# Four graph layers on one core: node stages without GpSimd, one sum accumulator, and VectorE reading one operand from PSUM beside indirect DMAs

## The chip, the cores and the metric

The kernel runs on one core of a Trainium2 chip. The metric is device time in microseconds (us), the median of the runs; lower is better. PE is TensorE, DVE VectorE, ACT ScalarE, POOL GpSimd, SP SyncE (it issues plain DMAs).

## The reference

A graph with 6250 nodes of 128 features and 100000 edges, sorted by destination, goes through four residual layers: `x = x + layer(relu(layernorm(x)))`.

```
layer 0  msg = x[dst] * fsum(edge);  agg = segment_sum(msg, src)
         out = gamma * (softplus(agg @ Wi1 + bi1) @ Wi2 + bi2 - mean) * rsqrt(var) + beta
layer 1  twice: h = x @ W; e = exp(leaky(h.a_src[src] + h.a_dst[dst]) - max)
         x = layernorm(x + segment_sum(h[src] * e / sum(e)) + bias) * gamma + beta
layer 2  m = segment_sum(relu([x[src], edge_attr, g] @ Wm1 + bm1) @ Wm2 + bm2) / degree
         out = layernorm(x + relu([x, m, g] @ Wu1 + bu1) @ Wu2 + bu2) * ln_g + ln_b
layer 3  as layer 1 once, with 8 heads of 16 features, no layernorm, + bias
```

In layers 1 and 3 each node also has an edge to itself, and the weights of a node's incoming edges sum to one.

## The kernel before

**Nodes.** They lie in SBUF as 52 tiles of 128 (`NBP`), in 13 groups of 4 (`NG`, `GN`): `X` is the residual, `XI` and `Y` are scratch, `ACC` and `H` have 136 words per node (`AW`). `H` holds the rows that go to the table in HBM.

**Edges.** Setup gives each edge a slot. The edges of one destination tile fill whole tiles of 128 slots, so the last tile of each is partly empty, and behind the last edge some tiles are wholly empty: 832 tiles (`NT`), in 104 halves of 8 (`G`). The record of a slot has the edge's attributes, its source node (`R_SRC`) and its places. Setup first fills all records from `pad_rec`; there the source of an empty slot is 0.

**Passes.** `layer0_dst_pass`: for each half DVE builds eight one-hot tiles (`onehot`, L1055) from `iota_row`, PE picks the node rows with them, DVE scales them (L1175), POOL scatters them by 8 indirect DMAs (L1267), SP stores the one-hots. At its end DVE adds `bn_shift` to `X` (L1204). `layer0_src_pass` sums those messages by source. `gat_pass` runs three times (layer 1 twice, layer 3), `mlp_pass` once: in each half POOL gathers 8 tiles of table rows by 8 indirect DMAs (L1359) into one of four buffers (`ring`, `DEEP`), waiting for PE's sum of four halves before; DVE waits for all 8, works out the logits (L1469 to L1475) and the previous half is added up (`add_sums`); ACT takes exp and, with one head, scales the rows (L1503); with 8 heads DVE multiplies the rows by the weights (L1481); PE sums by destination into PSUM. `add_sums` adds the 8 PSUM tiles alternately into `ACC` and `H` (`sums`, L1102), each add waiting for the one two before it. So every node stage behind a pass first adds `H` to `ACC`.

**Beside a pass.** Before the first half DVE runs `meanwhile`: in `gat_pass` it is `self_loops`, which scales `H` (the whole node table) by the self weights in `den` (L1673).

**Node stages.** `node_product` turns and multiplies 13 groups; DVE's part is `before(g)` (layer 1's second product: gamma and beta, L1753 and L1754) and `after`; SP stores the table rows; POOL runs `behind(g)` (L1667), which adds a bias to `XI` or `X`. Behind the two passes of layer 1 stands `end1`: DVE adds `H` to `ACC` for 32 tiles (L1780), then normalizes and adds `XI` tile by tile (L1782), and takes statistics of all 52 (L177), while POOL does the other 20 tiles (`pool1`). `mean2` (L1816, L1817) prepares layer 2's product. The last stage ends with `finish`: three operations (L1688, L1689, L1851) on each of four parts, three of 12 tiles on DVE and one of 16 on POOL, each followed by the part's DMA to the output.

The order between engines is set by semaphores alone; stages end with a barrier.

Of the kernel before, what the change touches and what calls it, by code (L numbers as in the profile page):

```python
# [25 lines left out]
P = 128  # L26
N = 6250
E = 100000
D = 128
# [62 lines left out]
def gnn(nc, a, out):  # L92
# [28 lines left out]
    with ctx:  # L121
# [33 lines left out]
        for v in ("L1_gnn_bias", "L1_gnn_gamma", "L1_gnn_beta"):  # L155
            for l in range(2):
                vec[v, l] = (sb(f"{v}{l}", [P, D]), a[v][l, :])
        mat = {"Wi1": (sb("Wi1", [P, D]), a["L0_gnn_Wi1"]), "Wi2": (sb("Wi2", [P, D]), a["L0_gnn_Wi2"]),
# [53 lines left out]
        def setup():  # L212
# [63 lines left out]
            with stage_of_work():  # L276
# [25 lines left out]
                NW = len(vec) + len(mat) + 7 + 9  # L302
                with nc.Block() as block:
                    @block.sync
                    def _(sp):
# [11 lines left out]
                        for t, v in vec.values():  # L317
                            sp.dma_start(t[:, :], v.unsqueeze(0).to_broadcast([P, D])).then_inc(weights_in, 16)
                        for t, v in mat.values():
                            sp.dma_start(t[:, :], v).then_inc(weights_in, 16)  # L320
# [52 lines left out]
                    def _(pool):  # L373
# [15 lines left out]
                        st.then(pool.memset(zero1[:, :], 0.0))  # L389
                        pool.sem_inc(consts, 1)  # L390
# [6 lines left out]
                        st.then(pool.memset(pr[:, :, R_POS:R_POS + 1], float(SKIP)))  # L397
                        st.then(pool.memset(pm[:, :, D:D + 1], -1.0))
# [347 lines left out]
        def per_col(t):  # L746

            return t[:, :].unsqueeze(1).to_broadcast([P, NBP, D])
# [344 lines left out]
        def add_sums(dve, n, q, places, tiles, w, summed, signals, added):  # L1093
# [14 lines left out]
        def layer0_dst_pass():  # L1108
# [9 lines left out]
            with nc.Block() as block:  # L1118
# [32 lines left out]
                def _(dve):  # L1151
# [33 lines left out]
                    dve.wait_ge(cleared, 2)  # L1185
# [18 lines left out]
                    nc.vector.tensor_tensor(X[:, :, :], X[:, :, :], per_col(bn_shift), ALU.add)  # L1204
# [68 lines left out]
        def layer0_src_pass():  # L1273
# [14 lines left out]
            with nc.Block() as block:  # L1288
# [40 lines left out]
                def _(dve):  # L1329
# [4 lines left out]
                        add_sums(dve, i * deep + q, q, two_sets, acc_of_s, D, summed, i * deep + q + 1, added)  # L1334
# [47 lines left out]
        def gat_pass(table, heads, meanwhile):  # L1382
# [10 lines left out]
            maxed, reduced, asked, exped, parts_ready, sums_cleared = (  # L1393
                sem(n) for n in ("maxed", "reduced", "asked", "exped", "parts_ready", "sums_cleared"))
# [23 lines left out]
            def picks(q):  # L1418

                return bank[q % 2][:, 0:G * 6 * heads]  # L1420

# [4 lines left out]
            with nc.Block() as block:  # L1426
# [24 lines left out]
                def _(dve):  # L1451
# [3 lines left out]
                    dve.wait_ge(exped, 1)  # L1455
                    meanwhile(nc.vector, then)
                    dve.wait_ge(sums_cleared, 1)

                    def half(r, q, n):
# [3 lines left out]
                        if known(n, 2):  # L1463
                            dve.wait_ge(probs, n - 1)
# [11 lines left out]
                        if known(n, 1):  # L1476
                            add_sums(dve, n - 1, q - 1, two_sets, acc_of_d, w, pe_done, n + 1, added)
                        if heads > 1:
                            dve.wait_ge(probs, n + 1)
# [6 lines left out]
                    add_sums(dve, HALVES - 1, DEEP - 1, two_sets, acc_of_d, w, pe_done, HALVES + 1, added)  # L1486

                @block.scalar
                def _(act):
                    for q in range(DEEP):  # L1490
                        copy_index(0, q, ix_ready)
                    nc.scalar.copy(ACC[:, :, :], zero1[:, :].unsqueeze(2).to_broadcast([P, NBP, AW])).then_inc(sums_cleared, 1)
                    act.wait_ge(asked, 1)
                    nc.scalar.activation(ps_self, ps_self, ACT.Exp, bias=zero1[:, :]).then_inc(exped, 1)
# [16 lines left out]
                def _(pe):  # L1511
# [14 lines left out]
                    def half(r, q, n):  # L1526
                        pe.wait_ge(logits, n + 1)
# [7 lines left out]
        def mlp_pass(table, meanwhile):  # L1535
# [10 lines left out]
            with nc.Block() as block:  # L1546
# [22 lines left out]
                def _(dve):  # L1569
                    def half(r, q, n):  # L1570
# [6 lines left out]
                        if known(n, 1):  # L1577
                            add_sums(dve, n - 1, q - 1, one_set, acc_of_d, w, summed, n, added)
# [6 lines left out]
                    add_sums(dve, HALVES - 1, DEEP - 1, one_set, acc_of_d, w, summed, HALVES, added)  # L1585
# [68 lines left out]
        def gat_product(l, heads, table, addends, normed, before=None):  # L1654
# [9 lines left out]
            def behind(g):  # L1664

                for t, row_vec in addends:
                    nc.gpsimd.tensor_tensor(t[:, group(g), :], t[:, group(g), :], columns(row_vec, GN), ALU.add)  # L1667
            node_product([XI], [wx[l]], after, before, normed, cols=cols, store=(table, H, D + heads), behind=behind)

        def self_loops(v, then, heads):  # L1670

            ps, h4 = by_head(den, heads), H[:, :, 0:D].rearrange("p b (k c) -> p b k c", k=heads)
            then(v.tensor_tensor(h4, h4, ps.unsqueeze(3).to_broadcast([P, NBP, heads, D // heads]), ALU.mult))  # L1673
            then(v.tensor_copy(H[:, :, D:D + heads], ps))

        def weights_of_nodes(v, then, heads):

            at = slice(D, D + heads)
            then(v.tensor_tensor(by_head(den, heads), ACC[:, :, at], H[:, :, at], ALU.add))  # L1679
            if heads == 8:  # L1680
                then(v.tensor_scalar(by_head(den, heads), by_head(den, heads), 1e-16, None, ALU.add))  # L1681
            then(v.reciprocal(by_head(den, heads), by_head(den, heads)))  # L1682

        def rows_of_nodes(v, then, tiles, heads):
# [3 lines left out]
            then(v.tensor_tensor(ACC[:, tiles, 0:D], ACC[:, tiles, 0:D], H[:, tiles, 0:D], ALU.add))  # L1688
# [67 lines left out]
        for l in range(2):  # L1756
            with stage_of_work():
                addends = [(XI, vec["L1_gnn_bias", l][0])]
                if l == 0:
                    gat_product(0, 1, tab_d[0], addends, relu_norm_x)  # L1760
                else:
                    addends.append((X, vec["L1_gnn_beta", 1][0]))
                    gat_product(1, 1, tab_d[1], addends, lambda g: scaled(g, ACT.Identity, Y), norm_l1)
                gat_pass(tab_d[l], 1, lambda v, then: self_loops(v, then, 1))
                weights_in_den = sem("weights_in_den")
                cut = NBP - 20
                assert cut % 2 == 0

                def pool1(pool, v, then):
                    tiles = slice(cut, NBP)  # L1770
                    then(v.tensor_tensor(ACC[:, tiles, 0:D], ACC[:, tiles, 0:D], H[:, tiles, 0:D], ALU.add))
                    pool.wait_ge(weights_in_den, 1)
                    then(v.tensor_tensor(ACC[:, tiles, 0:D], ACC[:, tiles, 0:D],
                                         by_head(den, 1)[:, tiles, :].to_broadcast([P, NBP - cut, D]), ALU.mult))
                    then(v.tensor_tensor(Y[:, tiles, :], ACC[:, tiles, 0:D], XI[:, tiles, :], ALU.add))

                def end1(d, v, then):
                    weights_of_nodes(v, then, 1)
                    d.dve.sem_inc(weights_in_den, 1)
# [118 lines left out]
```

## Time and profile before

| | us |
|---|---|
| time, median of 3 runs (lowest, highest) | 7642.42 (7634.22, 7653.16) |
| profiled execution: its own time | 7654.14 |
| its span in the trace | 7652.4 |
| busy in the span: PE, PEld, DVE, ACT, POOL | 3341.1, 2964.8, 3135.5, 1683.9, 5276.8 |
| TensorE clock granted, mean share of full speed | 0.636 |

PEld is TensorE's weight load. Busy time alone doesn't name a limit; what each stage waits for does. The stages by time of the trace: setup to about 1300, layer 0's destination pass to 2490, its source pass and product to 2857, then product and pass in turn: passes at 2897 to 3969, 4085 to 5155, 5267 to 6331 and 6507 to 7611, and the last node stage to the end.

### The profile page before, as it was taken

Reading aid. Unit: us, or ns where it says so; the run is one execution under the profiler, and the core shown is the slowest. Engines: PE = TensorE matmul, PEld = TensorE weight load, DVE = VectorE, ACT = ScalarE, POOL = GpSimd, SP = SyncE. Lnnn points to the kernel's source line nnn. Section 1 sums busy time; section 2 is a strip of 40 time slices with the busy share of each in tenths; the row PEclk is TensorE's granted clock in tenths of the full one; section 3 lists DMA queues with packets and bytes.
Section 4 is the critical chain, followed back from the end, with each engine's and each line's share of the span. In section 5 each row is a group of like instructions: output and inputs, shape, how many; then the busy total and the mean of one; then the engine's idle time right before and its main releaser. Section 6 shows DMA issues by size and latency. Waiting matters only on the chain. (4 is left out here: it accounts for less than half of the span.)

```text
span 7652.4 us, 88779 instructions
## 1 busy us (share of the span) xinstructions
PE 3341.1 (44%) x17325; PEld 2964.8 (39%) x17326; DVE 3135.5 (41%) x10255; ACT 1683.9 (22%) x4072; POOL 5276.8 (69%) x5234
## 2 busy tenths in 40 slices
PE   3100001444443764444434444444777675454543
PEld 1000001444443653444423444434666664344443
DVE  9777721222222663222244222225222326444444
ACT  3100000111111863222223222223222224000000
POOL 2677776777777737777756777764777770777775
PEclk9655555666666985555655555556777777566565
DMA  6122234444443624444443444453444451444444
GB/s 218 63 94 94 94 105 152 144 143 142 141 143 113 215 84 133 131 131 131 131 73 109 131 131 131 131 101 91 134 137 134 133 120 29 127 128 132 128 132 93
DMA packets 507506, 942.53 MB, mean 123 GB/s; under 512 B 204348, under 2 KB 240684, under 8 KB 507305
## 3 DMA queue, kind: packets, MB, share of 16 engines
q1 hardware_dynamic: 349288, 637.41, 24.8%
q0 software_dynamic: 158144, 304.31, 17.7%
q8 instruction: 26, 0.43, 0.0%
q14 instruction: 48, 0.39, 0.0%
HBM read 673.90 MB, written 270.84 MB: 123 GB/s over the span
## 5 line engine op out<-in xcount | busy, mean ns | idle before, releaser
L1359 POOL DMA_INDIRECT edge_buf<-node_table,ixr x1664 | 1614.4, 970 | 596.4 <-issue 506.7
L1359 POOL DMA_INDIRECT Y<-node_table,ixr x1664 | 1587.1, 954 | 507.4 <-issue 507.4
L1267 POOL DMA_INDIRECT layer_messages<-edge_buf,ixr x832 | 911.0, 1095 | 295.5 <-issue 263.8
L431 POOL DMA_INDIRECT edge_records<-edge_buf x782 | 792.2, 1013 | 255.6 <-issue 245.8
L1517 PE MATMUL bank<-adc,turned_buf 128*128 x2496 | 341.7, 194 | 1304.2 <-DVE z L1475 916.9
L1089 PE MATMUL bank<-edge_buf,Y 128*128 128x129 f32 (+2 forms) x3744 | 817.2, 404 | 213.4 <-ACT edge_buf L1503 104.8
L1469 DVE TENSOR_REDUCE pk<-bank 128x16 f32<-128x48 f32 (+1 forms) x312 | 101.3, 325 | 1883.4 <-DMA edge_buf<-node_table,ixr 946.2
L1089 PE MATMUL bank<-Y 128*128 128x129 f32 (+1 forms) x3328 | 758.3, 418 | 247.5 <-ACT Y L1503 130.1
L1089 PEld LDWEIGHTS bank<-edge_buf,Y 128*128 128x128 f32 x3744 | 756.1, 306 | 242.2 <-issue 120.2
L1517 PEld LDWEIGHTS bank<-adc,turned_buf 128*128 128x128 bf16 x2496 | 256.9, 103 | 1445.5 <-issue 1390.0
L1089 PEld LDWEIGHTS bank<-Y 128*128 128x128 f32 x3328 | 704.8, 319 | 271.0 <-issue 218.4
L1102 DVE TENSOR_TENSOR ACC<-ACC,bank 128x129 f32 (+2 forms) x2080 | 605.9, 291 | 354.8 <-issue 265.3
L1102 DVE TENSOR_TENSOR H<-H,bank 128x129 f32 (+2 forms) x2080 | 599.4, 288 | 3.2 <-DVE ACC L1102 1.7
L1215 PE MATMUL bank<-ident,Y 128*128 128x128 f32 x832 | 204.3, 427 | 821.2 <-DVE Y L1055 819.0
L1215 PEld LDWEIGHTS bank<-ident,Y 128*128 128x128 f32 x832 | 163.2, 223 | 845.0 <-issue 649.6
L1636 PE MATMUL bank<-wmbT,turned_buf 64*128 64x128 f32 x1664 | 312.2, 361 | 297.7 <-DVE Y L1575 148.4
L1636 PEld LDWEIGHTS bank<-wmbT,turned_buf 64*128 64x128 f32 x1664 | 285.6, 264 | 326.0 <-issue 301.2
L480 PE MATMUL bank<-Y,H 128*128 128x2 f32 (+1 forms) x6 | 1.4, 358 | 774.1 <-DVEq L708 774.1
L1498 ACT ACTIVATE edge_buf<-z,zero 128x8 f32<-128x8 f32 (+1 forms) x156 | 50.2, 322 | 1303.2 <-DVE z L1475 1303.2
L1227 PE MATMUL bank<-H,Y 128*128 x1664 | 329.8, 382 | 5.4 <-DVEq L1180 5.4
L1227 PEld LDWEIGHTS bank<-H,Y 128*128 128x128 f32 x1664 | 328.6, 302 | 5.6 <-issue 5.6
L1498 ACT ACTIVATE Y<-z,zero 128x8 f32<-128x8 f32 (+1 forms) x156 | 50.1, 321 | 1272.3 <-DVE z L1475 1272.3
(284 smaller groups left out, 5386.7 us busy)
## 6 DMA issues: line engine op xcount, KB each, us to landing
Y<-onehots SPq DMA_DIRECT2D x416, 512.0 KB
turned_buf<-onehots_turned SPq DMA_DIRECT2D x312, 256.0 KB
edge_buf<-edge_records SPq DMA_DIRECT2D x208, 288.0 KB
onehots<-Y SPq DMA_DIRECT2D x104, 512.0 KB, 2.7
layer_messages<-ACC SPq DMA_DIRECT2D x28, 1584.0 KB
XI<-layer_messages SPq DMA_DIRECT2D x78, 528.0 KB, 4.3
edge_records<-H SPq DMA_DIRECT2D x1, 29952.0 KB
onehots_turned<-turned_buf SPq DMA_DIRECT2D x104, 256.0 KB
```

Of the source, the lines that this page charges most:

```text
L431: pool.indirect_dma_start(rec_d, bass.IndirectOffsetOnAxis(ap=ixs[h][:, j:j + 1], axis=0), rec[h][:, j, :], None, bounds_check=SLOTS - 1, ...
L480: nc.tensor.matmul(bank[5][:, 16 * l:16 * l + 2 * heads_of[l]], wT[l], att[l], start=True, stop=True).then_inc(wT_ready, 1)
L1089: ins = nc.tensor.matmul(places.at(q, j, w), tiles_of_half(onehots)[:, j, :], messages[:, j, 0:w], start=True, stop=True)
L1102: nc.vector.tensor_tensor(acc, acc, places.at(q, j, w), ALU.add).then_inc(added, 1)
L1215: ins = nc.tensor.transpose(bank[j // 4][:, (j % 4) * P:(j % 4) * P + P], tiles_of_half(oh[h])[:, j, :], ident[:, :])
L1227: ins = nc.tensor.matmul(bank[2 + j // 4][:, (j % 4) * P:(j % 4) * P + P], ohT[h][:, j * P:j * P + P], Hflat[:, bass.ds(at[j] * AW, D)], s ...
L1267: pool.indirect_dma_start(msg_d, bass.IndirectOffsetOnAxis(ap=ixr[h][:, j:j + 1], axis=0), rows[h][:, j, 0:MW], None, bounds_check=SLOTS - ...
L1359: pool.indirect_dma_start(ring[q][:, j, 0:w], None, table, bass.IndirectOffsetOnAxis(ap=ixr[q][:, j:j + 1], axis=0)).then_inc(rows_in[q], 16)
L1469: st.then(nc.vector.tensor_reduce(ps, picks(q).rearrange("p (j t k) -> p j k t", j=G, t=3), AX.X, ALU.add))
L1498: nc.scalar.activation(ring[q][:, :, D:w], z[q % 2][:, :, 0:heads], ACT.Exp, bias=zero1[:, :]) \
L1517: ins = nc.tensor.matmul(picks(q)[:, j * 6 * heads:(j + 1) * 6 * heads], ohbT[q][:, j * P:j * P + P], adc[:, bass.ds(at[j] * (6 * heads), ...
L1636: ins = nc.tensor.matmul(bank[2 + j // 4][:, (j % 4) * P:(j % 4) * P + P], attrT[q % 2][:, j * P:j * P + P], wmbT[:, :], start=True, stop= ...
```

## The change

1. `onehot`, the add of `bn_shift` (L1204), `self_loops` (L1673) and the 8-head product (L1481) read one input from PSUM. Copies of `iota_row` and `bn_shift` are put in banks 4 and 5; ACT writes the self weights and, with 8 heads, each half's weights a second time, into PSUM. With 8 heads PE's pick of two halves on now waits for DVE's product.
2. `add_sums` is given its list of accumulators. In `gat_pass` and `mlp_pass` it is `ACC` alone, so each add waits for the one before it; layer 0's source pass keeps both. `self_loops` writes to `ACC`, ACT's clearing of `ACC` goes, and so do all adds of `H` to `ACC` behind these passes.
3. No node stage uses POOL. Layer 1's bias is added where `H` is copied from PSUM (`bias_row`); the additions to `X` are made by DVE beside the pass (`add_row_to_x`). `end1` and `finish` do all tiles on DVE, the last part of `finish` with 16 tiles.
4. In `pad_rec` the source of slot (p, j) is row 8p + j instead of 0, by one POOL iota in setup.

```diff
@@ setup
+                        st.then(pool.iota(pr[:, :, R_SRC:R_SRC + 1], [[1, G], [1, 1]], base=0, channel_multiplier=G,
+                                          allow_small_or_imprecise_dtypes=True))
@@ onehot, layer0_dst_pass
-            return nc.vector.tensor_tensor(tiles_of_half(oh[h]), iota_row[:, :].unsqueeze(1).to_broadcast([P, G, P]),
+            return nc.vector.tensor_tensor(tiles_of_half(oh[h]), bank[4][:, 0:P].unsqueeze(1).to_broadcast([P, G, P]),
...
+                    nc.vector.tensor_copy(bank[4][:, 0:P], iota_row[:, :]).then_inc(cleared, 1)
+                    nc.vector.tensor_copy(bank[5][:, 0:D], bn_shift[:, :]).then_inc(cleared, 1)
...
-                    nc.vector.tensor_tensor(X[:, :, :], X[:, :, :], per_col(bn_shift), ALU.add)
+                    nc.vector.tensor_tensor(X[:, :, :], X[:, :, :], per_col(bank[5][:, 0:D]), ALU.add)
@@ add_sums
-                acc = sums[j % 2][:, bass.ds(at[j], w)]
-                if j >= 2 or known(n, 1):
-                    dve.wait_ge(added, n * G + j - 1)
+                acc = accs[j % len(accs)][:, bass.ds(at[j], w)]
+                if j >= len(accs) or known(n, 1):
+                    dve.wait_ge(added, n * G + j + 1 - len(accs))
@@ gat_pass
-                            dve.wait_ge(probs, n + 1)
+                            dve.wait_ge(probs, (n + 1) * exps)
...
-                                                    ring[q][:, :, D:w].unsqueeze(3).to_broadcast([P, G, heads, c]),
+                                                    weights(q).unsqueeze(3).to_broadcast([P, G, heads, c]),
...
-                    nc.scalar.copy(ACC[:, :, :], zero1[:, :].unsqueeze(2).to_broadcast([P, NBP, AW])).then_inc(sums_cleared, 1)
...
+                        if heads > 1:
+                            nc.scalar.activation(weights(q), z[q % 2][:, :, 0:heads], ACT.Exp, bias=zero1[:, :]) \
+                                .then_inc(probs, 1)
...
-                        pe.wait_ge(logits, n + 1)
+                        pe.wait_ge(*((msg_ready, n + 1) if heads > 1 else (logits, n + 1)))
@@ gat_product
-                v.tensor_copy(H[:, at, 0:D + heads], rows_psum[:, :, 0:D + heads])
+                if l < 2:
+                    v.tensor_tensor(H[:, at, 0:D + 1], rows_psum[:, :, 0:D + 1],
+                                    bias_row[l][:, :].unsqueeze(1).to_broadcast([P, 2, D + 1]), ALU.add)
+                else:
+                    v.tensor_copy(H[:, at, 0:D + heads], rows_psum[:, :, 0:D + heads])
...
-                    nc.gpsimd.tensor_tensor(t[:, group(g), :], t[:, group(g), :], columns(row_vec, GN), ALU.add)
+        def add_row_to_x(v, then, row):
+            in_psum = bank[7][:, 0:D]
+            then(v.tensor_copy(in_psum, row[:, :]))
+            then(v.tensor_tensor(X[:, :, :], X[:, :, :], per_col(in_psum), ALU.add))
@@ self_loops
-            then(v.tensor_tensor(h4, h4, ps.unsqueeze(3).to_broadcast([P, NBP, heads, D // heads]), ALU.mult))
+            then(v.tensor_tensor(acc4, h4, ps_psum.unsqueeze(3).to_broadcast([P, NBP, heads, D // heads]), ALU.mult))
@@ end1
-                    then(v.tensor_tensor(ACC[:, 0:cut, 0:D], ACC[:, 0:cut, 0:D], H[:, 0:cut, 0:D], ALU.add))
-                    for b in range(cut):
+                    for b in range(NBP):
@@ layer 2: after_h, mlp_pass, mean2
-                v.memset(ACC[:, b:b + 2, :], 0.0)
-                v.tensor_tensor(X[:, b:b + 2, :], X[:, b:b + 2, :], columns(vec["L2_gnn_ln_b"][0], 2), ALU.add)
...
-            mlp_pass(tab_d[2], lambda v, then: then(v.memset(H[:, :, :], 0.0)))
+            def beside2(v, then):
+                then(v.memset(ACC[:, :, :], 0.0))
+                add_row_to_x(v, then, vec["L2_gnn_ln_b"][0])
+            mlp_pass(tab_d[2], beside2)
...
-                then(v.tensor_tensor(ACC[:, at, 0:D], ACC[:, at, 0:D], H[:, at, 0:D], ALU.add))
@@ last stage
-                    for n in range(3):
+                    for n in range(4):
                         finish(dve, nc.vector, then, n)
-                @block.gpsimd
-                def _(pool):
-                    pool.wait_ge(den_ready, 1)
-                    finish(pool, nc.gpsimd, Steps(pool, pool_steps).then, 3)
```

## Rows read from the trace of the kernel before

**Rows 1.** Windows: length; busy (x) PE, PEld, DVE, ACT, POOL; PE clock; DMA; GB/s.

```profile
1312.00:2489.00 1177.00, 506.09 (x2464) 483.90 (x2464) 326.72 (x618) 210.08 (x410) 910.99 (x832) 0.65 0.41 139
...
5267.00:6310.00 1043.00, 739.97 (x4112) 682.97 (x4112) 308.83 (x1018) 236.79 (x416) 787.25 (x832) 0.73 0.48 134
6506.00:7588.00 1082.00, 517.24 (x2464) 456.85 (x2464) 458.03 (x1435) 45.58 (x207) 826.51 (x833) 0.59 0.47 127
```

**Rows 2.** The scatters' source line: duration ns min/median/max; who waited for them (us, times).

```profile
L1267 POOL DMA_INDIRECT layer_messages<-edge_buf,ixr x832: 971/974/8733, 1312.7 to 2486.9; - x167
...
  DVE edge_buf L1168: 760.6, 102
```

**Rows 3.** Timeline of the destination pass, DVE and POOL: start us, duration us, engine, line.

```profile
1761.38 1.29 DVE L1175 TENSOR_TENSOR edge_buf<-bank,XI 128x512 f32<-128x512 f32 x2
1762.45 0.97 POOL L1267 DMA_INDIRECT layer_messages<-edge_buf,ixr  x1 [0.30 <-issue]
...
1763.54 1.22 DVE L1055 TENSOR_TENSOR Y<-iota_row,XI 128x1024 f32<-128x1024 f32 x1
1763.73 1.88 POOL L1267 DMA_INDIRECT layer_messages<-edge_buf,ixr  x1 [0.30 <-issue]
...
2462.51 8.73 POOL L1267 DMA_INDIRECT layer_messages<-edge_buf,ixr  x1 [0.30 <-DVE edge_buf L1175]
...
2463.32 7.07 DVE L1204 TENSOR_TENSOR X<-X,bn_shift 128x6656 f32<-128x6656 f32 x1
```

**Rows 4.** Timeline, start of layer 1's first pass and a half of layer 3's.

```profile
2900.16 7.09 DVE L1673 TENSOR_TENSOR H<-H,den 128x6656 f32<-128x6656 f32 x1
2900.28 7.79 POOL L1359 DMA_INDIRECT edge_buf<-node_table,ixr  x1 [0.30 <-issue]
...
7005.36 1.22 DVE L1481 TENSOR_TENSOR Y<-Y 128x1024 f32<-128x1024 f32 x1
7006.23 1.17 POOL L1359 DMA_INDIRECT Y<-node_table,ixr  x1 [0.30 <-issue]
```

**Rows 5.** Timeline, last gather of a half and DVE's start on it: mid-pass, then the end.

```profile
3403.68 0.94 POOL L1359 DMA_INDIRECT edge_buf<-node_table,ixr  x1 [0.30 <-issue]
...
3406.28 0.21 DVE L1469 TENSOR_REDUCE pk<-bank 128x16 f32<-128x48 f32 x1 [4.57 <-DMA edge_buf<-node_table,ixr]
...
3944.06 0.94 POOL L1359 DMA_INDIRECT Y<-node_table,ixr  x1 [0.30 <-issue]
...
3958.36 0.21 DVE L1469 TENSOR_REDUCE pk<-bank 128x16 f32<-128x48 f32 x1 [9.55 <-DMA Y<-node_table,ixr]
```

**Rows 6.** DMA queues, 3500 to 3600, then 3930 to 3960: packets, MB, share of 16 engines.

```profile
q0 software_dynamic: 2558, 5.29, 23.9%
...
q0 software_dynamic: 542, 1.10, 82.6%
```

**Rows 7.** Groups of the second layer-1 product, 4013 to 4073: busy us, mean ns, idle before.

```profile
L1753 DVE TENSOR_TENSOR XI<-XI,L_gnn_gamma 128x512 f32<-128x512 f32 x13 | 20.1, 1547 | 6.4 <-ACT XI L1695 4.8
...
L1754 DVE TENSOR_TENSOR XI<-XI,L_gnn_beta 128x512 f32<-128x512 f32 x13 | 18.4, 1416 | 0.4
```

**Rows 8.** `end1`: group of L1780, timeline of L1782, its durations (min/median/max ns).

```profile
L1780 DVE TENSOR_TENSOR ACC<-ACC,H 128x4096 f32<-128x4096 f32 x2 | 8.8, 4424 | 0.3
...
3973.85 23.49 DVE L1782 SCALAR_TENSOR_TENSOR Y<-ACC,den,XI 128x128 f32<-128x128 f32 x32
...
3985.57 11.51 DVE L1782 SCALAR_TENSOR_TENSOR Y<-ACC,den,XI 128x128 f32<-128x128 f32 x23
...
L1782 DVE SCALAR_TENSOR_TENSOR Y<-ACC,den,XI x64: 337/339/5736, 3973.9 to 5184.3; 128x128 f32<-128x128 f32 x64
```

**Rows 9.** The group that `mean2` loses.

```profile
L1816 DVE TENSOR_TENSOR ACC<-ACC,H 128x512 f32<-128x512 f32 x13 | 9.0, 691 | 2.3 <-PEq L761 0.5
```

**Rows 10.** Timeline of the last stage: L1851 on the first and the third part.

```profile
7618.45 5.94 DVE L1851 TENSOR_TENSOR X<-X,ACC 128x1536 f32<-128x1536 f32 x1
...
7641.03 1.76 DVE L1851 TENSOR_TENSOR X<-X,ACC 128x1536 f32<-128x1536 f32 x1
```

More of the change, by code:

```diff
@@ L154, in gnn @@
             vec[v] = (sb(v, [P, D]), a[v])
-        for v in ("L1_gnn_bias", "L1_gnn_gamma", "L1_gnn_beta"):
+        for v in ("L1_gnn_gamma", "L1_gnn_beta"):
             for l in range(2):
                 vec[v, l] = (sb(f"{v}{l}", [P, D]), a[v][l, :])
+        bias_row = [sb(f"L1_gnn_bias{l}", [P, D + 1]) for l in range(2)]
         mat = {"Wi1": (sb("Wi1", [P, D]), a["L0_gnn_Wi1"]), "Wi2": (sb("Wi2", [P, D]), a["L0_gnn_Wi2"]),
@@ L389, in _ @@
                         st.then(pool.memset(zero1[:, :], 0.0))
+                        for t in bias_row:
+                            st.then(pool.memset(t[:, D:D + 1], 0.0))
                         pool.sem_inc(consts, 1)
@@ L1652, in _, with gat_product @@
                     each_half(pe, half)
-        def gat_product(l, heads, table, addends, normed, before=None):
+        def gat_product(l, heads, table, normed, before=None):
             ad = by_head(a_dst, heads)
@@ L1670, in self_loops @@
+                then(v.tensor_copy(ad[:, at, :], rows_psum[:, :, D + heads:cols]))
+            node_product([XI], [wx[l]], after, before, normed, cols=cols, store=(table, H, D + heads))
+        def add_row_to_x(v, then, row):
+            in_psum = bank[7][:, 0:D]
+            then(v.tensor_copy(in_psum, row[:, :]))
+            then(v.tensor_tensor(X[:, :, :], X[:, :, :], per_col(in_psum), ALU.add))
         def self_loops(v, then, heads):
             ps, h4 = by_head(den, heads), H[:, :, 0:D].rearrange("p b (k c) -> p b k c", k=heads)
-            then(v.tensor_tensor(h4, h4, ps.unsqueeze(3).to_broadcast([P, NBP, heads, D // heads]), ALU.mult))
@@ L1674, in self_loops @@
-            then(v.tensor_copy(H[:, :, D:D + heads], ps))
+            acc4 = ACC[:, :, 0:D].rearrange("p b (k c) -> p b k c", k=heads)
+            ps_psum = bank[7][:, 0:NBP * heads].rearrange("p (b k) -> p b k", k=heads)
+            then(v.tensor_tensor(acc4, h4, ps_psum.unsqueeze(3).to_broadcast([P, NBP, heads, D // heads]), ALU.mult))
+            then(v.tensor_copy(ACC[:, :, D:D + heads], ps))
         def weights_of_nodes(v, then, heads):
-            at = slice(D, D + heads)
-            then(v.tensor_tensor(by_head(den, heads), ACC[:, :, at], H[:, :, at], ALU.add))
+            weights = ACC[:, :, D:D + heads]
@@ L1680, in weights_of_nodes @@
             if heads == 8:
-                then(v.tensor_scalar(by_head(den, heads), by_head(den, heads), 1e-16, None, ALU.add))
-            then(v.reciprocal(by_head(den, heads), by_head(den, heads)))
+                then(v.tensor_scalar(by_head(den, heads), weights, 1e-16, None, ALU.add))
+                weights = by_head(den, heads)
+            then(v.reciprocal(by_head(den, heads), weights))
         def rows_of_nodes(v, then, tiles, heads):
@@ L1687, in rows_of_nodes @@
             acc4 = ACC[:, tiles, 0:D].rearrange("p b (k c) -> p b k c", k=heads)
-            then(v.tensor_tensor(ACC[:, tiles, 0:D], ACC[:, tiles, 0:D], H[:, tiles, 0:D], ALU.add))
             then(v.tensor_tensor(acc4, acc4, by_head(den, heads)[:, tiles, :].unsqueeze(3)
@@ L1757, in gnn, with beside1 @@
             with stage_of_work():
-                addends = [(XI, vec["L1_gnn_bias", l][0])]
                 if l == 0:
-                    gat_product(0, 1, tab_d[0], addends, relu_norm_x)
+                    gat_product(0, 1, tab_d[0], relu_norm_x)
                 else:
[L1762 to L1775, printed above, removed]
+                    gat_product(1, 1, tab_d[1], lambda g: scaled(g, ACT.Identity, Y), norm_l1)
+                def beside1(v, then):
+                    self_loops(v, then, 1)
+                    if l == 1:
+                        add_row_to_x(v, then, vec["L1_gnn_beta", 1][0])
+                gat_pass(tab_d[l], 1, beside1)
                 def end1(d, v, then):
                     weights_of_nodes(v, then, 1)
-                    d.dve.sem_inc(weights_in_den, 1)
-                    then(v.tensor_tensor(ACC[:, 0:cut, 0:D], ACC[:, 0:cut, 0:D], H[:, 0:cut, 0:D], ALU.add))
-                    for b in range(cut):
+                    for b in range(NBP):
                         ins = v.scalar_tensor_tensor(Y[:, b, :], ACC[:, b, 0:D], den[:, b:b + 1], XI[:, b, :], ALU.mult, ALU.add)
                     then(ins)
-                    for b in range(cut):
-                        ins = count_stats(v, b, Y)
-                    d.wait_pool()
-                    for b in range(cut, NBP):
+                    for b in range(NBP):
                         ins = count_stats(v, b, Y)
@@ L1790, in end1 @@
                     finish_stats(v, then, d.root)
-                Dense(end1, roots=1, on_pool=pool1)
+                Dense(end1, roots=1)
                 if l == 1:
@@ L1840, in gnn, with beside3 @@
         with stage_of_work():
-            gat_product(2, 8, tab_d[3], [(X, vec["L3_gnn_bias"][0])], relu_norm_x)
-            gat_pass(tab_d[3], 8, lambda v, then: self_loops(v, then, 8))
-            den_ready, written, steps, pool_steps = (sem(n) for n in ("den_ready", "written", "steps", "pool_steps"))
+            gat_product(2, 8, tab_d[3], relu_norm_x)
+            def beside3(v, then):
+                self_loops(v, then, 8)
+                add_row_to_x(v, then, vec["L3_gnn_bias"][0])
+            gat_pass(tab_d[3], 8, beside3)
+            written, steps = sem("written"), sem("steps")
             parts = [slice(n * GN * 3, (n + 1) * GN * 3) for n in range(3)] + [slice(GN * 9, NBP)]
```

40 lines of the change are left out of this document (21 added, 19 removed).

## The prediction, made before the changed kernel ran

> **What bounds the kernel now.** I read the windows first, to see which engine each stage keeps busy, then the timeline for what that engine does there. In layer 0's destination pass POOL is busy 911 of 1177 us, in the MLP pass 787 of 1043, in the 8-head pass 827 of 1082; no other engine comes near in the first and last [rows 1]. The timeline tells what fills POOL's rest: 0.30 us of issue between one indirect DMA and the next, and no wait for anyone [rows 3, 4]. So a pass lasts as long as POOL takes for 832 DMAs: 0.974 + 0.30 us each for a scatter [rows 2], 787.25/832 = 0.946 + 0.30 for a gather [rows 1]. DVE has room: in the destination pass it waits 761 us for scatters to land, 7.5 us in each of 102 halves [rows 2]. Between the passes DVE sets the pace. The change therefore pays only where it shortens one of POOL's DMAs, what follows the last of them, or DVE's own list in a node stage.
>
> **POOL held up by DVE.** One scatter in eight is long. The one that starts at 1763.73 beside a one-hot (two inputs in SBUF) takes 1.88 us and ends 0.85 us after it; the one that starts at 1762.45 while L1175 runs (one input PSUM) takes its ordinary 0.97 [rows 3]. The same holds for L1673, 7.09 us long, with a gather of 7.79, for L1481, and for L1204 [rows 3, 4]. The reading: a DMA whose start falls into a DVE operation with two SBUF inputs waits for its end, one beside a PSUM input doesn't.
> - Destination pass: 910.99 - 832 x 0.974 = 100.6 us over the plain length. Of it 8.73 - 0.97 = 7.8 is L1204's; a short cast in front of it may keep some 0.7, the pass's first DMA another 0.6. Saved: 99 us, 92 of it by the one-hots.
> - `self_loops`: 7.79 - 0.95 = 6.8 us in each of three passes, 20.5 us.
> - 8-head product: 826.51 - 787.25 (the MLP pass, which has no such operation) = 39.3; less 0.4 for the reduction in that window, 6.8 counted above and about 2 for small operations at the start that stay: 30 us.
>
> Bounds: all of it as long as one PSUM input is enough, nothing if it isn't. I take the upper end, since L1175 is the same form of operation (PSUM times SBUF) and ran 208 times in this very pass. The new copies into PSUM and the second exp stand where DVE and ACT wait, 0.2 to 0.6 us each. One sentence from the Trainium skill speaks against it: "SBUF — State Buffer", Who interferes with whom, names a contention between two SBUF inputs and GpSimd instructions that read SBUF, but infers that a tensor_tensor leaves the writing of DMA descriptors alone. By that the long DMAs would have another cause and these 149.5 us stay; the rows with L1055 and L1673 disagree with it, and go before it.
>
> **The end of each pass.** Mid-pass DVE starts 3406.28 - (3403.68 + 0.94) = 1.66 us after a half's last gather; at the end 3958.36 - 3945.00 = 13.36 us [rows 5]. There the queue moves 1.10 MB in 30 us at 82.6% of the DMA engines' time, mid-pass 5.29 MB in 100 us at 23.9% [rows 6]: 5 times the time per byte. The last tiles are all empty slots, so every read goes to row 0. With different rows I expect the mid-pass lag: 11.7 us saved at each of four passes, 46 us. Bounds: nothing (rows a fixed step apart no better), 47. Mid-pass the slow reads of partly empty tiles are hidden behind POOL's issue and give nothing.
>
> **One accumulator.** Adds now follow each other. Two on different buffers start 0.21 us apart while one takes 0.29; dependent ones would start about 0.32 apart (0.29 and the 0.03 seen between dependent DVE operations). Eight: 0.9 us more. In a pass this goes into DVE's 7 us of waiting; on the path are six groups of eight (the last of the layer-1 passes, two each for the MLP and 8-head passes, where PE's sum or the product stands behind the adds): -5.3 us. Bounds: 0 to -14 (0.5 us apart). The 7 us add to `X` beside three passes delays the first half by up to 6 us, and four buffers of 10 us hide that; without that cover it would be 6 us each. ACT's clearing of `ACC` ended before it was needed.
>
> **Node stages.**
> - Layer 1's second product: L1753 and L1754 take 38.5 us for 26 operations beside POOL's additions [rows 7]; L1816, the same shape, needs 0.691 [rows 9]. 38.5 - 18.0 = 20.5 us. Bounds 15 (ACT, or the store of the table, is late next) and 26. The other products are paced by ACT and gain nothing.
> - `end1`: gone are L1780 (4.4 us) and 23.5 us for 32 L1782, three of them stuck behind POOL for up to 5.7; in come 52 at (11.51 - 5.74)/22 = 0.262 us, 13.6 [rows 8]. With the small add at its head 14.6 us, twice: 29 us. Bounds 27 and 30.
> - `mean2` loses 13 x 0.72 (0.691 and the gap) = 9.4 us, as DVE works there without a break [rows 9]. Bounds 6 and 9.4.
> - End: nine operations of 1536 columns, three of which POOL stretches from 1.76 to 5.0 or 5.9 [rows 10], about 27.4 us; then six of 1.76 and two of 2048 columns at about 2.3, 15.2 us. With fewer tiles behind the last of them to be sent, 14 us. Bounds 10 and 18.
>
> **Sum.** 99 + 20.5 + 30 + 46 - 5.3 + 20.5 + 29 + 9.4 + 14 = 263 us. The profiled execution took 7654.1 us, 11.7 above the median of its runs, so 7391 for one like it and 7642.4 - 263 = **7379 us** for the median.
>
> **The rivals.**
> - PSUM doesn't free POOL: the output or the remaining SBUF input is what blocks. For it: only small or half-length PSUM operations were seen beside POOL. Against it: 208 of L1175 without one long DMA that needs them. The 149.5 us stay: 7529 us. Chance 0.07. The inference quoted from the Trainium skill's "SBUF — State Buffer" would lead here.
> - Empty slots stay slow at a pass's end: the new rows stand 8 apart, a step near 4 KB in each table, and could meet in one part of HBM. Against it: mid-pass rows are spread at random and come at once, and 128 different rows can hardly be as bad as one. 46 us stay: 7425 us. Chance 0.08.
> - Slower: the dependent add. DVE's half in the 8-head pass is about 3.7 us and eight adds, in the layer-1 passes 2; in the MLP pass PE's sum (near 4 us) waits for the adds. From an add every 0.8 us (1.0 in layer 1) DVE and not POOL would pace all 416 halves, and from 0.96 it eats the whole gain; at 1.0 the time is about 7379 + 8 x 0.2 x 208 = 7712 with what the ends lose. For it: each add has a wait on a count in a register and an address from a register. Against it: they have both now, and start 0.21 us apart. Chance 0.03.
> - Something that no row shows, among it that nothing changes: 0.02.
>
> **How the numbers follow.** My forecast has 0.80, with 7355 to 7420 as its own range. The full range takes in the empty slots' case: 7340 to 7440; it leaves out the first and third rival. Within 0.3% (23 us, about what a measurement of this kernel tells from none) only partial failures of several kinds would end: 0.02. Slower 0.03, faster 0.95.
>
> **What would show it.** In the destination pass no scatter of 1.9 us, POOL's busy time near 812 us, the pass 1077 us long; in the 8-head pass POOL near 789; no gather of 7.8. At each pass's end DVE within 2 us of the last gather. L1753's successor at 0.69, 52 STT 0.26 apart, POOL absent between passes. It is wrong if long DMAs remain beside the one-hots, if adds start more than 0.5 us apart, or if POOL waits for PE's sums.

## The result and the profile after

The changed kernel takes **7409.4 us** (median of 4 runs, 7404.5 to 7412.4) against 7647.7 us (4 runs, 7634.2 to 7653.2): a ratio of 0.9688, interval 0.9677 to 0.9700, 238 us less. Predicted were 7379 us, 263 us less, with a range of 7340 to 7440. The profiled execution took 7404.5 us, span 7402.5: 249.9 us of span less than the profiled one of before. That difference is accounted for here, stretch by stretch, from the start of the first and the end of the last indirect DMA of each pass. The column "expected" puts the prediction's own terms into the stretches.

| stretch | before, us | after, us | difference | expected |
|---|---|---|---|---|
| start to first setup scatter | 242.2 | 250.5 | +8.3 | 0 |
| setup scatters, to first destination scatter | 1070.6 | 1069.4 | -1.2 | 0 |
| destination pass | 1175.1 | 1073.2 | -101.9 | -99 |
| to first gather of layer 1 | 409.7 | 411.7 | +2.0 | 0 |
| layer-1 passes | 1047.5, 1047.4 | 1038.5, 1038.3 | -9.0, -9.2 | -6.8 each |
| between them | 140.5 | 85.5 | -55.0 | -46 |
| second to MLP pass | 135.1 | 108.4 | -26.6 | -25 |
| MLP pass | 1040.7 | 1038.2 | -2.5 | 0 |
| MLP to 8-head pass | 198.4 | 174.9 | -23.6 | -19 |
| 8-head pass | 1079.5 | 1057.8 | -21.7 | -37 |
| last gather to the end | 65.8 | 56.1 | -9.6 | -24 |

Two stretches gave less than expected, the 8-head pass with what follows it and the start. Two gave clearly more: those in front of the second layer-1 pass and of the 8-head pass, where POOL begins with an all-reduce.

The windows of the destination, MLP and 8-head pass answer to [rows 1]:

```profile
1319.00:2394.00 1075.00, 494.82 (x2464) 473.51 (x2464) 327.00 (x619) 210.21 (x410) 809.29 (x832) 0.66 0.44 152
5075.00:6114.00 1039.00, 791.27 (x4144) 720.02 (x4144) 374.57 (x1027) 237.53 (x415) 784.95 (x832) 0.68 0.46 135
6288.00:7347.00 1059.00, 481.32 (x2440) 434.47 (x2440) 513.33 (x1429) 70.36 (x309) 786.56 (x833) 0.66 0.46 132
```

POOL's busy time in the first row is 809 where it was 911, in the third 787 where it was 827. But the third window is 20 us longer than the second at the same POOL work: POOL now waits there. The source line of the scatters (durations in ns: min, median, max) and the timeline beside a one-hot answer to [rows 2, 3]:

```profile
L1279 POOL DMA_INDIRECT layer_messages<-edge_buf,ixr x832: 969/972/1742, 1319.9 to 2392.2; - x167
```

```profile
1755.68 1.23 DVE L1064 TENSOR_TENSOR Y<-bank,XI 128x1024 f32<-128x1024 f32 x1
1755.94 0.97 POOL L1279 DMA_INDIRECT layer_messages<-edge_buf,ixr  x1 [0.30 <-issue]
...
2807.46 7.09 DVE L1702 TENSOR_TENSOR ACC<-H,bank 128x6656 f32<-128x6656 f32 x1
2807.58 0.95 POOL L1371 DMA_INDIRECT edge_buf<-node_table,ixr  x1 [0.30 <-issue]
```

The operations on DVE have the shapes and the lengths that they had (1.22 and 7.09 us, [rows 3, 4]). One input now comes from a bank, and the DMA that starts inside them takes 0.97 or 0.95 us, not 1.88 or 7.79. At the end of the first layer-1 pass, for [rows 5, 6]:

```profile
3842.39 0.94 POOL L1371 DMA_INDIRECT Y<-node_table,ixr  x1 [0.30 <-issue]
3844.97 0.21 DVE L1486 TENSOR_REDUCE pk<-bank 128x16 f32<-128x48 f32 x1 [5.15 <-DMA Y<-node_table,ixr]
...
3846.66 0.29 DVE L1111 TENSOR_TENSOR ACC<-ACC,bank 128x129 f32 x1 [0.64 <-issue]
```

```profile
q0 software_dynamic: 384, 0.79, 11.3%
```

DVE begins 1.64 us after the last gather, 13.36 before. The second view is the gathers' DMA queue from 3830 to 3858 (packets, MB, share of 16 engines). Share times window over MB gives 4.0 us for each MB; in the rows of before it is 4.5 mid-pass and 22.5 at the end. The groups of the second layer-1 product, then `end1`, then the first and last part of the last stage, for [rows 7, 8, 10]:

```profile
L1781 DVE TENSOR_TENSOR XI<-XI,L_gnn_gamma 128x512 f32<-128x512 f32 x13 | 9.0, 692 | 6.4 <-ACT XI L1723 4.8
L1782 DVE TENSOR_TENSOR XI<-XI,L_gnn_beta 128x512 f32<-128x512 f32 x13 | 9.0, 692 | 0.4
```

```profile
3857.09 13.74 DVE L1800 SCALAR_TENSOR_TENSOR Y<-ACC,den,XI 128x128 f32<-128x128 f32 x52
...
7381.79 1.76 DVE L1869 TENSOR_TENSOR X<-X,ACC 128x1536 f32<-128x1536 f32 x1
...
7393.43 2.29 DVE L1869 TENSOR_TENSOR X<-X,ACC 128x2048 f32<-128x2048 f32 x1
```

**Where the 8-head pass is bound now.** Two halves of it on DVE, PE and POOL:

```profile
7007.92 3.29 DVE L1111 TENSOR_TENSOR ACC<-ACC,bank 128x136 f32 x8 [4.19 <-PE bank L1098]
...
7011.12 1.21 DVE L1498 TENSOR_TENSOR edge_buf<-edge_buf,bank 128x1024 f32<-128x1024 f32 x1
...
7013.34 1.11 PE L1538 MATMUL bank<-adc,turned_buf 128*128 x8 [5.56 <-DVE edge_buf L1498]
...
7014.46 3.62 PE L1098 MATMUL bank<-edge_buf,Y 128*128 128x136 f32 x16
...
7018.22 3.29 DVE L1111 TENSOR_TENSOR ACC<-ACC,bank 128x136 f32 x8 [4.41 <-PE bank L1098]
...
7019.03 0.94 POOL L1371 DMA_INDIRECT edge_buf<-node_table,ixr  x1 [0.66 <-issue]
```

Read the releasers in brackets: the adds wait for PE's sums, the picks for the product, the product for the adds in front of it. That is a closed ring: adds 3.29, product 1.21 (it begins at the last add's end), 1.0 until PE picks, picks 1.12, sums 3.62, 0.14 until the next adds; 10.3 us from one half's adds to the next. From the eleventh half to the last few the products follow each other in 10.16 to 10.31 us, 10.24 in the mean. POOL needs 8 x (0.944 + 0.305) = 9.99. The ring is slower and first uses up the slack of the four buffers. After that POOL has to wait at the first DMA of a half, where its gap grows from 0.30 to as much as 0.69. Over the pass POOL's gaps sum to 271.6 us against 253.4 before. These first gaps make up 8.8 of the 18.2 us more. The rest comes in front of the second DMA of a half, nearly all of it in holes of 1.86 us that stand at every twelfth half from half 38 on. Holes of 1.84 to 1.88 us stand at every 112th scatter of the destination pass too, in both kernels. What makes any of them the traces don't tell; the ring keeps its 10.24 us through them. In before's trace eight adds took 1.79 us and the picks ran beside them.

### The profile page after: what moved, and what is told of

Read it like the earlier page. It is cut to its first block and busy times, and to the rows that moved or that the text cites. A ratio compares the mean times of both kernels' runs of the same rounds, so it can differ in the third digit from the quotient of the medians.

```text
span 7402.5 us, 89274 instructions
## 1 busy us (share of the span) xinstructions
PE 3331.8 (45%) x17325; PEld 2957.3 (40%) x17326; DVE 3299.0 (45%) x10231; ACT 1691.6 (23%) x4176; POOL 5000.4 (68%) x5176
## 5 line engine op out<-in xcount | busy, mean ns | idle before, releaser
L1371 POOL DMA_INDIRECT edge_buf<-node_table,ixr x1664 | 1571.6, 944 | 619.4 <-issue 507.9
L1371 POOL DMA_INDIRECT Y<-node_table,ixr x1664 | 1569.7, 943 | 521.1 <-issue 519.9
L1111 DVE TENSOR_TENSOR ACC<-ACC,bank 128x129 f32 (+2 forms) x3744 | 1092.9, 292 | 1102.2 <-PE bank L1098 469.2
L1279 POOL DMA_INDIRECT layer_messages<-edge_buf,ixr x832 | 809.3, 973 | 295.7 <-issue 263.0
L1657 PE MATMUL bank<-wmbT,turned_buf 64*128 64x128 f32 x1664 | 293.0, 345 | 192.3 <-DVE Y L1596 101.3
L1657 PEld LDWEIGHTS bank<-wmbT,turned_buf 64*128 64x128 f32 x1664 | 266.7, 248 | 224.6 <-issue 210.1
L1267 ACT COPY Y<-bank 128x512 f32<-128x512 f32 x208 | 123.8, 595 | 840.3 <-PE bank L1239 840.1
L1177 DVE COPY edge_buf<-XI 128x8 f32 (+1 forms) x104 | 18.7, 180 | 664.6 <-DMA layer_messages<-edge_buf,ixr 664.6
```

The source lines that it names most:

```text
L1177: nc.vector.tensor_copy(rows[h][:, :, D:D + 1], fields[:, bass.ds(t, G), R_SLOC - EA:R_SLOC - EA + 1]) \
L1267: nc.scalar.copy(ohT[h][:, at], bank[n][:, :]).then_inc(ohT_ready, 1)
L1279: pool.indirect_dma_start(msg_d, bass.IndirectOffsetOnAxis(ap=ixr[h][:, j:j + 1], axis=0), rows[h][:, j, 0:MW], None, bounds_check=SLOTS - ...
L1371: pool.indirect_dma_start(ring[q][:, j, 0:w], None, table, bass.IndirectOffsetOnAxis(ap=ixr[q][:, j:j + 1], axis=0)).then_inc(rows_in[q], 16)
L1657: ins = nc.tensor.matmul(bank[2 + j // 4][:, (j % 4) * P:(j % 4) * P + P], attrT[q % 2][:, j * P:j * P + P], wmbT[:, :], start=True, stop= ...
```

## The experiments

Experiments 1 to 4 ran on one chip (before there: 7651.8 us), the others on a second (7636.3), but for the all-reduce at the end in experiment 6, which ran on a third. There the kernel before takes 8980.7 us, and in that run POOL's gaps in a gather pass sum to 399 to 456 us and not 253; why that chip is slower was not looked into. So ratios are compared. Gathers take 0.944 us in some executions and 0.947 in others, with either kernel, which makes 2.0 to 2.5 us a pass; POOL's sums are compared with this in mind. Whole times step too: of experiment 1's four runs the profiled one, with 0.944, took 7367.6 us and the others 7383.0 to 7384.8; of experiment 7's five the profiled one, with 0.947, took 7368.6 and the others 7353.0 to 7354.4.

**1. Only the picks go back in front of the product.** For that the weights move to PSUM banks that the picks don't use.

```diff
-                return bank[q % 2][:, 384:384 + G * heads].rearrange("p (j k) -> p j k", k=heads)
+                return bank[4 + 3 * (q % 2)][:, 384:384 + G * heads].rearrange("p (j k) -> p j k", k=heads)
-                        pe.wait_ge(*((msg_ready, n + 1) if heads > 1 else (logits, n + 1)))
+                        pe.wait_ge(logits, n + 1)
```

> The changed kernel, with the 8-head weights moved from the picks' PSUM bank to one that the sums of the same half use, so that PE picks the half after next as soon as the logits are out again, ahead of the product. Theory (a ring: product on DVE, pick and sums on PE, eight dependent adds on DVE, 10.17 us a half against POOL's 9.97): the ring loses the pick's 1.15 us and falls below POOL, so the 8-head pass goes from 1057.8 to 1038-1042 us and the time from its last gather to the last add from 30.4 to 22-26; in all 20 to 26 us less than the 7409.4 of the changed kernel, about 7386. Rival (ACT's second exp, or something in POOL's own issue, makes the gaps): pass and total stay at 1058 and 7409.

Measured: 7383.4 us, ratio 0.9649 (0.9633 to 0.9665). Pass 1040.1 us, from the last gather to the last add 15.9 us (30.1 in the changed kernel; 24.0 before). The window of the pass:

```profile
6283.00:7324.00 1041.00, 512.06 (x2472) 453.16 (x2473) 529.02 (x1449) 71.03 (x312) 787.23 (x833) 0.60 0.46 134
```

```profile
7007.85 3.29 DVE L1111 TENSOR_TENSOR ACC<-ACC,bank 128x136 f32 x8 [0.80 <-issue]
7007.96 1.13 PE L1538 MATMUL bank<-adc,turned_buf 128*128 x8 [1.30 <-DVE z L1492]
...
7011.05 1.21 DVE L1498 TENSOR_TENSOR Y<-Y,bank 128x1024 f32<-128x1024 f32 x1
...
7012.36 3.97 PE L1098 MATMUL bank<-Y 128*128 128x136 f32 x16 [3.27 <-DVE Y L1498]
```

The picks run beside the adds, the sums follow the product by 0.1 us, and the adds no longer wait for PE. ACT's second exp and the slow adds are still there, so neither of them alone holds the pass up. The holes of 1.86 us are gone as well, here and in experiment 2. The ring had cost 17.7 us in the pass and 14.2 behind it.

**2. Only two accumulators again, in the 8-head pass.**

```diff
+            accs = sums if heads > 1 else sums[0:1]
-                            add_sums(dve, n - 1, q - 1, two_sets, sums[0:1], acc_of_d, w, pe_done, n + 1, added)
+                            add_sums(dve, n - 1, q - 1, two_sets, accs, acc_of_d, w, pe_done, n + 1, added)
                 self_loops(v, then, 8)
+                then(v.memset(H[:, :, :], 0.0))
```

with `H` added to `ACC` again behind the pass.

> The changed kernel, with two accumulators again in the 8-head pass alone (H cleared ahead of the pass, added in at the end: some 6 us of clearing that the buffers may hide, 0.6 and four times 1.8 us of adding behind the pass). Theory (the ring): adds start 0.21 us apart instead of 0.43, a half's ring is 8.7 us, POOL paces again: pass 1038-1042 us instead of 1057.8, from the last gather to the last add 24 to 26 us instead of 30.4, less 16 to 24 and plus 8, about 7395. Rival (pick behind the product is enough by itself to pace the pass): pass 1050 us or more, total 7409 or above.

Measured: 7389.2 us, ratio 0.9655 (0.9639 to 0.9671). Pass 1042.0 us, adds 0.21 us apart:

```profile
7024.10 0.30 DVE L1111 TENSOR_TENSOR ACC<-ACC,bank 128x136 f32 x1 [0.83 <-issue]
7024.31 0.29 DVE L1111 TENSOR_TENSOR H<-H,bank 128x136 f32 x1
...
7027.93 1.14 PE L1539 MATMUL bank<-adc,turned_buf 128*128 x8 [5.05 <-DVE Y L1499]
```

The late picks alone do no harm either. It takes both edits. Of the ring's 10.3 us the slow adds are 1.5 and the late picks 2.1; without either one it lies below POOL's 9.99 us.

**3. The kernel before, with only the one-hots' iota in PSUM.**

```diff
+                    nc.vector.tensor_copy(bank[4][:, 0:P], iota_row[:, :]).then_inc(cleared, 1)
-            return nc.vector.tensor_tensor(tiles_of_half(oh[h]), iota_row[:, :].unsqueeze(1).to_broadcast([P, G, P]),
+            return nc.vector.tensor_tensor(tiles_of_half(oh[h]), bank[4][:, 0:P].unsqueeze(1).to_broadcast([P, G, P]),
```

> The kernel before, with one edit: the one-hots of layer 0's destination pass take iota from PSUM. Theory (a DVE operation with two SBUF inputs holds up POOL's DMA, one PSUM input frees it): no scatter of 1.88 us is left but the one beside L1204, the pass goes from 1175 to about 1083 us, in all 92 us less: 7556. Rival (the output or the remaining SBUF input is what blocks, and the changed kernel gains elsewhere): 7648.

Measured: 7559.9 us, ratio 0.9878 (0.9861 to 0.9894). The pass took 1082.3 us, 92.8 less:

```profile
1313.00:2397.00 1084.00, 507.35 (x2464) 484.89 (x2464) 327.18 (x617) 209.88 (x409) 817.79 (x832) 0.66 0.44 151
```

```profile
L1268 POOL DMA_INDIRECT layer_messages<-edge_buf,ixr x832: 971/974/8736, 1313.6 to 2394.9; - x167
```

Of 100.6 us over the plain length 7.4 are left; the scatter beside the addition to `X` still takes 8.74 us. So where one operand lies decides. Its length, its output and its other input are as they were.

**4. The kernel before, with only different rows in the empty slots.**

```diff
+                        st.then(pool.iota(pr[:, :, R_SRC:R_SRC + 1], [[1, G], [1, 1]], base=0, channel_multiplier=G,
+                                          allow_small_or_imprecise_dtypes=True))
```

> The kernel before, with one edit: empty slots name 1024 different rows instead of row 0. Theory (one row read by all is slow, different rows are not): DVE starts 1.7 us after the last gather at all four pass ends instead of 13.4, 46 us less: 7602. Rival (the ends got shorter through the other edits): 7648. On the start: the changed kernel's POOL stood still for 9.3 us at its second instruction; if this iota brings that about, the first setup scatter comes at 250 us and not at 242.

Measured: 7603.4 us, ratio 0.9935 (0.9918 to 0.9951), 48 us less. DVE starts 1.6 to 1.7 us after the last gather at all four ends:

```profile
3942.22 0.95 POOL L1361 DMA_INDIRECT Y<-node_table,ixr  x1 [0.31 <-issue]
3944.78 0.21 DVE L1471 TENSOR_REDUCE pk<-bank 128x16 f32<-128x48 f32 x1 [6.64 <-DMA Y<-node_table,ixr]
```

The first setup scatter comes at 242.1: this iota has nothing to do with the changed kernel's late start.

**5. One row for each DMA of a half.** As 4, with `channel_multiplier=0`.

> The kernel before, with one edit: empty slots name eight different rows, by their tile in the half, so that all 128 of a DMA's reads still go to one row, but the eight DMAs of a half to eight. If what is slow is the reading of one row by all 16 engines, DVE starts less late than 13.4 us where DMAs overlap: with one row a DMA I expect 5 to 13 us after the last gather; with no difference between rows (rows of a table as near as these meet in one place), 13.4. If only the whole queue's meeting in a single row were slow, 1.7.

```profile
3937.75 0.94 POOL L1361 DMA_INDIRECT Y<-node_table,ixr  x1 [0.30 <-issue]
3941.54 0.21 DVE L1471 TENSOR_REDUCE pk<-bank 128x16 f32<-128x48 f32 x1 [6.79 <-DMA Y<-node_table,ixr]
```

Measured: DVE starts 2.6 to 2.9 us after the last gather at the four ends. I had expected 5 to 13. There is one run, of 7601.5 us, too few to read a difference in time from. All 128 reads of a DMA in one row cost only 1.2 us; what cost 11.7 was a queue of DMAs that all read the same one.

**6. The start and the all-reduces.** POOL's first instructions in the changed kernel:

```profile
0.80 0.20 POOL L380 MEMSET ident<- 128x128 f32 x1 [0.29 <-POOLq L1898]
10.55 0.28 POOL L381 TENSOR_SCALAR_AFFINE_SELECT ident<-ident 128x128 f32<-128x128 f32 x1 [9.54 <-issue]
```

Before, the select starts at 1.49. And the all-reduce in front of the second layer-1 pass, first before, then after:

```profile
4076.66 0.25 DVE L1398 TENSOR_REDUCE gmax<-H 128x1 f32<-128x52 f32 x1 [4.27 <-PEq L822]
...
4084.98 0.38 POOL L1445 PARTITION_ALL_REDUCE gmax_all<-gmax  x1 [8.65 <-issue]
```

```profile
3927.69 0.24 DVE L1410 TENSOR_REDUCE gmax<-H 128x1 f32<-128x52 f32 x1 [3.59 <-PEq L831]
...
3928.09 0.39 POOL L1463 PARTITION_ALL_REDUCE gmax_all<-gmax  x1 [84.76 <-DVEq L1411]
```

The 8 us are gone there and in front of the 8-head pass, and stay in front of the first layer-1 pass (2795.94 to 2804.27), where POOL's last work was 104 TENSOR_TENSOR instructions in layer 0's source pass. In the traces POOL's sequencer has a MODIFY_POOL_CONFIG pair at its start, with or without a standstill there, and wherever its work changes between all-reduce and TENSOR_TENSOR, and nowhere else. In the kernel before, POOL's parts of `end1` and of the last stage start 6.8, 6.9 and 7.1 us behind such a pair too. That led to a theory: POOL holds the code of one kind of instruction, and a swap costs 7 to 9 us. Two edits on top of experiment 1, and one on the kernel before, test it. The first, in the last stage:

```diff
+                @block.gpsimd
+                def _(pool):
+                    nc.gpsimd.tensor_tensor(gmax[:, :], gmax_all[:, :], gmax_all[:, :], ALU.add)
```

> The changed kernel with the early pick (7383.4 us), and one small POOL addition in the last stage, beside DVE's work there. Theory (POOL keeps the code it ran last, an all-reduce needs another one than additions and selects, a swap takes 7 to 9 us, and an execution starts with what the last one left): the swap happens at the end, where POOL has nothing to do, and the 9.0 to 9.3 us standstill at POOL's first select is gone; first setup scatter at 242 instead of 250 us, in all 8 us less, about 7375. The addition waits some 7 us for the swap, DVE's last work takes 19: nothing is lost there. Rival (the standstill comes from the size or place of the changed kernel's code): the first scatter stays at 250 us, total 7383.

Measured: 7360.4 us, ratio 0.9637 (0.9622 to 0.9652). First setup scatter at 242.1, and

```profile
1.49 0.29 POOL L381 TENSOR_SCALAR_AFFINE_SELECT ident<-ident 128x128 f32<-128x128 f32 x1 [0.49 <-POOL ident L380]
```

The second, early in the first layer-1 product, beside DVE's and PE's work:

```diff
+                    nc.gpsimd.partition_all_reduce(gmax_all[:, 0:1], zero1[:, :], P, bass.bass_isa.ReduceOp.max)
```

> The changed kernel with the early pick (7383.4 us), and one all-reduce of a column of zeros on POOL early in the first layer-1 product, whose result nobody uses. Theory (swap of POOL's code): POOL swaps beside the product, the real all-reduce of that stage starts at once and not 8.3 us late, from the last destination scatter to the first gather 403 us instead of 411.4, in all 8 us less, about 7375. Rival (the all-reduce itself takes 8 us the first time, or waits for something of DVE): the real one is late as before, total 7383.

Measured: 7362.0 us, ratio 0.9639 (0.9624 to 0.9654); from the last scatter to the first gather 404.3 us (411.4 in experiment 1):

```profile
2769.70 0.38 POOL L1682 PARTITION_ALL_REDUCE gmax_all<-zero  x1 [106.24 <-DVEq L814]
2796.47 0.39 POOL L1463 PARTITION_ALL_REDUCE gmax_all<-gmax  x1 [26.40 <-DVEq L1411]
```

The first waited 6.6 us for its swap, beside the product; the real one ran as soon as it was asked for. The ratios of these two runs lie 0.0012 and 0.0010 below experiment 1's, with intervals that overlap, so it is the places in the trace that show the effect, and not the times.

The third, the kernel before with an all-reduce as POOL's last work:

```diff
                     finish(pool, nc.gpsimd, Steps(pool, pool_steps).then, 3)
+                    pool.partition_all_reduce(gmax_all[:, :], gmax[:, :], P, bass.bass_isa.ReduceOp.max)
```

> The kernel before, with one all-reduce as POOL's very last work, behind its additions of the last stage and beside the sending of the output, where it costs nothing. Theory (an execution starts with the code that the last one left on POOL): now this kernel too stands still for some 9 us at POOL's first select, the first setup scatter comes at about 250 us and not 242, and the time is 8 us above before. Rival (the standstill belongs to the changed kernel's own code): 242 us, and no change.

Measured: 8991.4 against 8980.7 us, ratio 1.0014 (1.0004 to 1.0023). First setup scatter at 250.0, and

```profile
10.28 0.28 POOL L376 TENSOR_SCALAR_AFFINE_SELECT ident<-ident 128x128 f32<-128x128 f32 x1 [9.27 <-issue]
```

So an execution starts with the state that the last one left. The kernel before ended with additions on POOL and started ready; the changed kernel ends with nothing on POOL since the all-reduce, and pays at its next start. The interval of this run's time (4 to 21 us) holds the 8; the trace shows it at its place. The Trainium skill, "GPSIMD Engine Reference", Instruction dispatch, says that `ModifyPoolConfig` can load new code and that the first call pays some 6 us; the traces agree in kind, with 5.7 (the all-reduce at the end) to 9.3 us. That the state outlives an execution stands on these runs. That the state is loaded code is my reading: they show the standstill, when it comes and how to move it, and not what POOL does meanwhile.

**7. All of it together:** experiment 1 and both edits.

> Both of the two edits before on the changed kernel with the early pick (7383.4 us). Theory: 16 to 17 us less, about 7367. Rival: neither does anything, 7383.

Measured: 7353.6 us (5 runs), ratio **0.9628** (0.9615 to 0.9641). It beats both kernels, by 46 us the changed one if its ratio is carried over (0.9688 - 0.9628 = 0.0060 of 7648).

## Why the prediction was right, and where it was off

- **POOL held up by DVE** (predicted 149.5 us): right. POOL's time over the plain length fell from 100.6 to 0.6 us in the destination pass and from 38.2 to 0.7 in the 8-head pass; in the layer-1 passes 6.3 and 6.5 are gone. Together 150.4. Experiment 3 shows the cause on the one-hots alone; for the other operations the trace after shows the plain DMA beside them. The Trainium skill's "SBUF — State Buffer", Who interferes with whom, infers that a tensor_tensor leaves descriptor writing alone; taken as a forecast for these DMAs, experiment 3 goes against it. The rule of the same section that the prediction names beside it, two SBUF inputs against GpSimd instructions that read SBUF, fits all of these rows, if an indirect DMA counts as one: each reads its row numbers from `ixr` in SBUF. Whether that reading is held up or the writing of descriptors, no run here separates.
- **The end of each pass** (46): right in mechanism, by experiment 4 (48 us as a whole). In the changed kernel it paid at three passes, 11.3 to 12.0 us each. At the fourth the ring of the 8-head pass stood behind the gathers and hid it.
- **One accumulator** (-5.3): the step that failed is "dependent ones would start about 0.32 apart", and with it "in a pass this goes into DVE's 7 us of waiting". They start 0.427 apart, inside its bounds of 0.5: each add's register operation for its wait runs only when the add before has ended, 0.04 us later, and takes 0.05. In the layer-1 and MLP passes the waiting did take it up; in the 8-head pass it did not, as experiment 2 shows. A group of eight costs 1.5 us and not 0.9; the four groups in front of the second layer-1, MLP and 8-head passes 2.4 us more than expected.
- **The picks behind the product.** This edit was in the diff and not in the sum: the prediction costed the second exp and not PE's new wait on `msg_ready`, nor who waits behind it. With the adds it made the ring, 18.4 us of gaps in the pass and 14.2 us behind it. The third rival looked for the same failure, DVE and PE instead of POOL as the pace, but set its threshold at an add every 0.8 us. It counted each engine's work by itself and not the chain that runs through both; with the picks in the chain 0.43 was enough.
- **Node stages:** right. Second layer-1 product 21.7 us (predicted 20.5), `end1` 14.6 twice (14.6), `mean2` 8.8 (9.4), of which DVE's next wait for PE takes back 1.3, the last stage 12.9 on DVE and 2.8 in what is left to send (14).
- **Not foreseen:** POOL's standstills. From DVE's last copy of the node stage to the first gather it took 8.4 us less in front of the second layer-1 pass (0.7 of it because the barrier no longer waits for POOL's additions) and 6.6 less in front of the 8-head pass, and the start took 8.3 more. In before's timeline the all-reduces stand 6.5 to 8.1 us behind the DVE operation that they wait for; I had taken that for their cost.

The sum: 263 expected, less 32.6 for the ring (18.4 and 14.2), less 8.3 for the start, plus 15.0 for the two all-reduces, plus some 13 because the profiled execution has the shorter DMA times (832 x 0.003 in each of four passes, 1.6 in the setup and 1.7 in the destination pass), gives 250; the spans differ by 249.9. Smaller terms, among them the 2.4 us of adds and 2.0 more in front of the first layer-1 pass, cancel. That the time came so near the forecast is in part luck: 40.9 us were lost in places that the sum had at nothing or too low, and 15.0 were gained in one that it did not have. The medians differ by 238, as before's profiled execution stood 6.5 us above its median and the one after 4.9 below. What makes an indirect DMA 3 ns longer in some executions stays open.

## What to carry to other kernels

When an edit adds a wait to an engine or lengthens a dependent run, add up the closed chain through all engines from one iteration to the next and compare it with the pace-setter's period; each engine's free time alone says nothing. Beside indirect DMAs give DVE's two-input operations one operand in PSUM, and let padding slots name different rows. Keep POOL to one kind of work on the critical path, or let it change kind beside other engines' work, and look at what it ends with: the next execution starts with that.

## What the runs showed of the hardware

- One PSUM operand in a DVE operation of 1.2 or 7.1 us takes an indirect DMA beside it from 1.88 or 7.79 us to 0.97 or 0.95.
- Where the last gathers of a pass all read one row, DVE starts 12.4 to 13.7 us after the last of them in the kernel before (8.8 to 10.9 on the third chip); with one row for each DMA, eight in all, 2.6 to 2.9; with different rows 1.5 to 1.9.
- A change between POOL's all-reduce and its TENSOR_TENSOR or select instructions costs 5.7 to 9.3 us, and the state outlives the execution.
- A dependent add whose wait goes through a register starts 0.13 us after the one before has ended; dependent operations that wait on a constant follow in 0.03.
- PE's first pick started 0.8 to 1.0 us after the product that it waited for. Before, its sums, on the same kind of wait, followed in 0.2, and in experiment 1 in 0.1; why the picks are slower to start was not tried.
